# Graph attention on one core: maxima over two rounds, V over dead K, three banks of sums

## The reference

```python
q = (feats @ Wq.T + bq).reshape(bs, NHEAD, HDIM).transpose(1, 0, 2)   # k, v alike
qe = q[:, c, :]; ke = k[:, r, :]; ve = v[:, r, :]                     # one row per edge
sim = jnp.einsum('hed,hed->eh', qe, ke) * scale
m = jax.ops.segment_max(sim, c, num_segments=bs)                      # per node and head
p = jnp.exp(sim - m[c])
s = jax.ops.segment_sum(p, c, num_segments=bs)
attn = p / s[c]
agg = jax.ops.segment_sum(attn.T[..., None] * ve, c, num_segments=bs) # reshaped to 256
return agg @ Wo.T + bo
```

## Time and profile before

| What | Value |
|---|---|
| Median of three runs | 6950.24 us (6938.55 to 6957.0) |
| The profiled execution | 6949.4 us |
| Its span, first to last instruction | 6947.6 us |
| First `product` (L1670) | starts at 3812.0 us |
| Last `product` | starts at 6702.6 us |
| Last `add` (L1716) | starts at 6742.6 us |
| Busy over the whole span | PE 65%, DVE 65%, ACT 57%, POOL 67% |

### The profile page before, as it was taken

One profiled execution on the slowest core, in us unless ns is written; L12 is line 12 of the kernel. 1 busy time (PEld: TensorE's weight loads), 2 busy tenths in 40 slices (PEclk: granted clock), 3 DMA queues, 4 the chain that ended last, 5 costly groups with the idle time before them and its releaser, 6 DMA issues. The chain is left out here.

```text
span 6947.6 us, 117508 instructions
## 1 busy us (share of the span) xinstructions
PE 4531.6 (65%) x19717; PEld 3355.2 (48%) x19717; DVE 4539.1 (65%) x12295; ACT 3956.7 (57%) x14482; POOL 4638.8 (67%) x3716
## 2 busy tenths in 40 slices
PE   1366666666666666664886677777677777777767
PEld 1344444444444545543553555555555555555545
DVE  4565555555556666663554777777777777777766
ACT  0665555555555555552332667677676767677661
POOL 1478888888888888887554566666666666666630
PEclk6677777777777777776998888888888888788889
DMA  8767777777777777778774566666666666676746
GB/s 314 188 105 106 104 107 106 106 107 106 106 106 109 107 109 107 110 108 184 263 260 144 167 183 190 188 195 187 199 190 198 197 196 201 199 206 202 206 145 196
DMA packets 644181, 1130.07 MB, mean 163 GB/s; under 512 B 74529, under 2 KB 466795, under 8 KB 643445
## 3 DMA queue, kind: packets, MB, share of 16 engines
q0 software_dynamic: 367600, 678.97, 49.7%
q1 hardware_dynamic: 223985, 273.78, 12.1%
q10 hardware_dynamic: 51860, 169.74, 7.4%
HBM read 929.80 MB, written 451.51 MB: 199 GB/s over the span
## 5 line engine op out<-in xcount | busy, mean ns | idle before, releaser
L701 POOL DMA_INDIRECT sums<-mtw,posIw x1563 | 2489.4, 1593 | 599.1 <-issue 408.2
L1249 POOL DMA_INDIRECT kv<-kvt,sI x1760 | 1763.8, 1002 | 1044.0 <-ACT room L1613 654.3
L1613 ACT ACTIVATE room<-kv,pp 128x33 f32<-128x33 f32 x8800 | 1918.1, 308 | 42.3 <-issue 38.1
L1528 PE MATMUL ps<-room,Of 128*128 128x264 f32 x3520 | 1143.0, 467 | 611.5 <-issue 339.3
L734 PE MATMUL ps<-h,wf 128*128 x3320 | 1212.0, 518 | 303.3 <-DVE mtw L825 230.6
L718 PE MATMUL ps<-Mw,Oh 128*128 128x128 f32 x3320 | 672.7, 368 | 926.9 <-DVE Oh L852 926.9
L825 DVE SCALAR_TENSOR_TENSOR mtw<-mtw,cont,ps 128x256 f32 x1660 | 794.2, 478 | 619.2 <-SPq L690 452.1
L1528 PEld LDWEIGHTS ps<-room,Of 128*128 128x128 f32 x3520 | 727.3, 224 | 890.7 <-issue 618.2
L718 PEld LDWEIGHTS ps<-Mw,Oh 128*128 128x128 f32 x3320 | 630.1, 274 | 1041.7 <-DVE Oh L852 1011.7
L734 PEld LDWEIGHTS ps<-h,wf 128*128 128x128 f32 x3320 | 805.8, 260 | 590.8 <-issue 455.3
L799 ACT COPY wf<-ps 128x512 f32<-128x512 f32 x415 | 242.7, 585 | 1238.8 <-PE ps L718 870.3
(11 more groups left out here) (223 smaller groups left out, 4509.3 us busy)
## 6 DMA issues: line engine op xcount, KB each, us to landing
qb<-qt SPq DMA_DIRECT2D x880, 192.0 KB
accd<-acc SPq DMA_DIRECT2D x880, 132.0 KB
ints<-srows ACTq DMA_DIRECT2D x205, 512.0 KB
OT<-drows SPq DMA_DIRECT2D x110, 512.0 KB
sums<-zero ACTq DMA_DIRECT2D x72, 704.0 KB
part<-sums SPq DMA_DIRECT2D x56, 896.0 KB
kv<-kvt,sI POOLq DMA_INDIRECT x1760
kvt<-kvo SPq DMA_DIRECT2D x98, 260.0 KB
```

The source lines that it names most:

```text
L701: e.indirect_dma_start(sums[t % NS], bass.IndirectOffsetOnAxis(ap=posI[:, t % NP:t % NP + 1], axis=0), mt[:, t % NM, :], None, compute_op= ...
L1249: e.indirect_dma_start(kv[:, s % NK, :], None, kvt, bass.IndirectOffsetOnAxis(ap=sI[:, s:s + 1], axis=0)).then_inc(kvs.sem(s), 16)
L1528: m = e.matmul(psum[6 + j % 2][:, 0:NH * 33], lhsT=Of[:, w % 2, k % W2, :], rhs=pv[:, k % NV, :], start=(k % 2 == 0), stop=(k % 2 == 1))
L1613: e.activation(pv[:, s % NV, h * 33:h * 33 + 33], kv[:, s % NK, D + h * 33:D + h * 33 + 33], ACT.Copy, scale=pp[:, w % 2, h, s % W2:s % W2 ...
```

## The change

It does five things, all in the attention stage.

1. **The chain takes two rounds.** `turn` of round w-1 and `spread` of round w-2 share PE's step u = 0; `ends` of w-1, `back` and `factor` of w-2 share u = 2. DVE does `inner` of w-1 and `outer` of w-2 at u = 1, `across` of w-1 at u = 3. ACT takes `exps` of w-2, the tops of w-1 and the factor of w-2 at u = 3, and a copy of the transposed similarities (`zs`) and the limits at u = 1. `sims` has three places in place of two.
2. **One bank for the chain.** All its results lie in bank 4, so PE waits before it writes there until ACT has read what lay there. ACT now copies the transposed similarities (`zs`) and the factor (`fac`) to SBUF, two new copies per round; the scans and `rescale` read these.
3. **Later weighing.** Weighing of quad Q comes in step Q+11, `agg` in Q+12, `add` in Q+13 (STEPS = 440 + 13).
4. **Three banks of sums.** Banks 5, 6 and 7: `agg` of sum j waits for the `add` of sum j-3.
5. **V on dead K.** `kv` is 12 columns of 7 x 264 floats. Successive rows of one column lie 264 floats lower, so that a row's V covers the K of the row gathered 12 slots before. The gather of quad g waits for the product of quad g-3, and for the weighing of quad g-15. 12 slots are gathered ahead of the stage, in place of 24. ACT raises its semaphore once per slot, not once per head, and POOL no longer waits row by row.

```diff
-        NK, NQ, RB, NE = 44, 8, 8, 24
+        NQ, RB = 8, 8
+        CH, VP, HW = 12, 6, NH * 33
+        NE = CH
...
+        kvs = Ring(sw[0:11], 4)
...
+        def lot(s):
+
+            return VP - s // CH % VP
+
+        def keys(s, n):
+            return kv[:, s % CH:s % CH + n, lot(s) * HW - D:lot(s) * HW]
+
+        def values(s, n):
+            return kv[:, s % CH:s % CH + n, lot(s) * HW:(lot(s) + 1) * HW]
 
         def gather(e, s):
 
-            e.indirect_dma_start(kv[:, s % NK, :], None, kvt, bass.IndirectOffsetOnAxis(
+            e.indirect_dma_start(kv[:, s % CH, lot(s) * HW - D:(lot(s) + 1) * HW], None, kvt, bass.IndirectOffsetOnAxis(
                 ap=sI[:, s:s + 1], axis=0)).then_inc(kvs.sem(s), 16)
 
...
-                e.wait_ge(S("l_wact"), NH * weighed(1, Q))
+                e.wait_ge(S("l_wact"), weighed(1, Q))
...
                                         ALU.mult).then_inc(S("l_wpool"), 1)
 
                 e.iota(icolI[:, :], pattern=[[0, 1]], base=0, channel_multiplier=1).then_inc(S("l_iota"), 1)
-                for g in range(NQD + 10):
-                    if g >= 10:
-                        weigh(g - 10)
-                    if g < NQD:
-                        if g >= NK // 4:
-                            wait_weighed(e, g - NK // 4)
-                        for s in range(max(NE, 4 * g), 4 * g + 4):
-                            if g >= NK // 4 and s % 4:
-                                before = NH * weighed(1, g - NK // 4)
-                                e.wait_ge(S("l_wact"), before + s % 4 * NH * len(shares(g - NK // 4 + 1)[1]) // 4)
+                for g in range(NQD + 14):
+                    if g >= 14:
+                        weigh(g - 14)
+                    if CH // 4 <= g < NQD:
+                        e.wait_ge(S("l_prod"), g - CH // 4 + 1)
+                        if g >= (VP - 1) * CH // 4:
+                            wait_weighed(e, g - (VP - 1) * CH // 4)
+                        for s in range(4 * g, 4 * g + 4):
                             gather(e, s)
 
...
-                        if j >= 2:
-                            e.wait_ge(S("l_add"), j - 1)
+                        if j >= 3:
+                            e.wait_ge(S("l_add"), j - 2)
                         for k in (2 * j, 2 * j + 1):
-                            m = e.matmul(psum[6 + j % 2][:, 0:NH * 33], lhsT=Of[:, w % 2, k % W2, :], rhs=pv[:, k % NV, :],
+                            m = e.matmul(psum[5 + j % 3][:, 0:NH * 33], lhsT=Of[:, w % 2, k % W2, :], rhs=pv[:, k % NV, :],
                                          start=(k % 2 == 0), stop=(k % 2 == 1))
                         m.then_inc(S("l_summed"), 1)
...
                 for p in range(STEPS):
                     w, u = p // 4, p % 4
-                    if u == 0:
-                        factor(w - 2)
                     expand(p + 1)
                     if u == 0:
+                        if 0 <= w - 2 < NW2:
+                            e.wait_ge(S("l_top"), w - 1)
+                        if 0 <= w - 3 < NW2:
+                            e.wait_ge(S("l_pp"), w - 2)
+                            e.wait_ge(S("l_fac"), w - 2)
                         turn(w - 1)
-                    elif u == 1:
+                        spread(w - 2)
+                    elif u == 2:
+                        if 0 <= w - 1 < NW2:
+                            e.wait_ge(S("l_z"), w)
+                        if 0 <= w - 2 < NW2:
+                            e.wait_ge(S("l_lim"), w - 1)
                         ends(w - 1)
-                    elif u == 2:
-                        spread(w - 1)
-                    else:
-                        back(w - 1)
-                    agg(p - 8)
+                        back(w - 2)
+                        factor(w - 2)
+                    agg(p - 12)
...
                         for h in range(NH):
-                            e.activation(pv[:, s % NV, h * 33:h * 33 + 33],
-                                         kv[:, s % NK, D + h * 33:D + h * 33 + 33], ACT.Copy,
-                                         scale=pp[:, w % 2, h, s % W2:s % W2 + 1]).then_inc(S("l_wact"), 1)
-
...
+                            m = e.activation(pv[:, s % NV, h * 33:h * 33 + 33], from_row[:, h * 33:h * 33 + 33], ACT.Copy,
+                                             scale=pp[:, w % 2, h, s % W2:s % W2 + 1])
+                        m.then_inc(S("l_wact"), 1)
...
+
+                def factor(v):
+                    if 0 <= v < NW2:
+                        e.wait_ge(S("l_factor"), v + 1)
+                        if v:
+                            e.wait_ge(S("l_rescale"), v)
+                        e.copy(fac[:, :], chain[:, fcol]).then_inc(S("l_fac"), 1)
+
+                def turned(v):
+                    if 0 <= v < NW2:
+                        e.wait_ge(S("l_ts"), v + 1)
+                        if v >= 2:
+                            e.wait_ge(S("l_bw2"), v - 1)
+                        e.copy(zs[:, v % 2, :], chain[:, zcol]).then_inc(S("l_z"), 1)
...
+                for p in range(STEPS):
+                    w, u = p // 4, p % 4
+                    if u == 3:
+                        if 0 <= w - 1 < NW2:
+                            e.wait_ge(S("l_tops"), w)
+                        if 0 <= w - 2 < NW2:
+                            e.wait_ge(S("l_factor"), w - 1)
+                        exps(w - 2)
+                    weigh(p - 11, 0)
+                    if u == 1:
+                        if 0 <= w - 2 < NW2:
+                            e.wait_ge(S("l_sides"), w - 1)
+                        turned(w - 1)
+                        limits(w - 2)
+                    if u == 3:
+                        ends(w - 1)
+                        factor(w - 2)
+                    weigh(p - 11, 1)
...
-                    add(p - 9, 0)
+                    add(p - 13, 0)
                     reduce(p)
-                    add(p - 9, 1)
+                    add(p - 13, 1)
+                    weigh(p - 11)
                     if u == 0:
                         columns(w + 1)
-                        rescale(w - 2)
+                        onehots(w - 2, 0)
+                        rescale(w - 3)
+                    elif u == 1:
                         inner(w - 1)
-                    elif u == 1:
-                        weigh(p - 7)
+                        outer(w - 2)
+                    elif u == 2:
+                        onehots(w - 2, 1)
+                    else:
                         across(w - 1)
-                    elif u == 2:
-                        weigh(p - 7)
-                        onehots(w - 1, 0)
-                        outer(w - 1)
-                    else:
```

91 lines of the change are left out of this document (41 added, 50 removed).

## The result

Over four runs each the changed kernel takes 7127.66 us (7096.73 to 7142.33) and the kernel before 6951.26 (6938.55 to 6957.0): a ratio of 1.025, with a 95% interval of 1.021 to 1.029. The forecast was 6566 us. The profiled execution took 7096.73 us, its span 7094.8.

A forecast was written before the change was run, and what follows sets the result against it. No engine is full; late PE results hold the 26.5 us round, above POOL's 21.0 us floor. Forecast: 6949.4 - 418 (110 rounds, 26.5 to 22.7 us) + 35 for the stage's ends = 6566 us, range 6390 to 6880.

The forecast's parts named there:

- the waits before the scans: DVE's idle time before across, inner and outer, 310.5 us or 3.2 us per round, was to go.
- the slack of the sums: Three banks give PE's two sums per step 7.2 and 5.1 us to spare; a 9.1 us delay leaves 4.0 idle.
- I price them at nothing: PE's new waits on ACT were to cost nothing; if ACT runs a step later, add waits up to 5.1 us.
- R: The new round of the attention stage, taken as 22.7 us where it was 26.5; its range 21.8 to 23.7.
- the fill: Start of the stage: with 12 slots gathered ahead, not 24, the first quads save less, costing +16 us.
- The drain: End of the stage: four more quads of weighing at 4.7 us of ACT each, +19 us.
- The floor: POOL's lowest round: 16 gathers 1.25 us apart and one weighing, 21.0 us.
- the case in which delays vanish: Rival: no delay of PE's results passes its slack, so R is 21.0 us and time 6379 us; chance 0.15.
- The one in which waits move to the sums in every round: Rival: every round has one 9.1 us delay on the sums, R 24.3 us, time 6742 us; chance 0.24.
- The slower rival, the gate of the gathers: Rival: POOL, at most three quads ahead, stands 5.7 us per round for the product; R 26.7, 7006 us; chance 0.12.
- The delay that I couldn't explain: PE's results reach ACT 6.3 and DVE 9.1 us late while gathers stream, and come through when POOL pauses.
- The rule on two SBUF operands: DVE instructions with two SBUF inputs and POOL's weighing shut each other out, about 0.5 us per round; left out of the sum.

The follow-up runs named there:

- chip 4: Another chip with held results, where the changed kernel was rerun against the kernel before: 7123.55 us beside 7003.57, ratio 1.0168.
- chip 7: A chip where nothing is held, where the changed kernel was run against the kernel before: 6428.96 us beside 6350.44, ratio 1.0129.
- lead2: Changed kernel with gathers waiting for the product two quads ahead, not three: 7165.88 us, against 7123.55 for the changed kernel on that chip.

## Why the prediction was wrong

**Right: the waits before the scans go.** 310.5 us before, none now.

**The step that failed: the slack of the sums, and "I price them at nothing".** I gave each sum at least 5.1 us to spare, the first of a step 7.2, against a delay of 9.1 us, and so 4.0 us of waiting in half of the rounds. I priced PE's new order at nothing, since behind the chain's matmuls "stands only `agg`". That was the point. In PE's step u = 2 the two sums now come behind `ends`, `back` and `factor`, and these wait for the scans at the end of DVE's step u = 1 (L1847 ends at 5011.90 in the timeline above, the sums start at 5013.14). I had the first sum of a step end 1.0 us before the start of the product; in this step it ends 2.5 us after it. From the records of the trace (4000 to 6600 us), each `add` set beside its own sum: the first `add` of DVE's step u = 3, which needs that sum, has a median slack of 3.3 us. It waits over 1 us in 71 of 94 rounds, 6.8 us on average, and starts then a median of 11.6 us after PE is done. This one `add` per round has 484 of the 599 us. In all, 83 of 94 rounds wait over 1 us at some `add`, 7.2 us on average. So three sizes were off: the slack (3.3, not 7.2 or 5.1), the delay (11.6, not 9.1) and how often (nearly all rounds, not half). And I had no term for the product: 1.4 us a round. Measured are 6.4 us before `add` and 1.4 before the product; with 20.1 us of work they make the 28.0 us.

**In the sum.** R is 27.96 in place of 22.7 us, which is 110 x 5.26 = 578 us. The ends gave 48 us less than I had (below). 6566 + 578 - 48 = 7096 is the profiled execution; the median of the four runs lies 31 us higher, which makes up the miss of 562.

**What `pp` is not.** ACT's 699.3 / 93 = 7.5 us a round before `pp` look like the cause, since the weighing of a round follows directly behind. But of the 598.6 us that DVE waited before `add`, 598.5 came after PE had finished the sum (by the modelled ends of matmuls), and a sum started a median of 2.4 to 10 us after its quad had been weighed, by its place in the round. On chip 4, 458 of 471 us came after. So the late weighing isn't what DVE waited for. ACT has 19.1 us of work in a round of 28, and rests where its order makes it wait. No run gave `pp` or the sums of u = 2 more slack, so this rests on the accounts of the traces and not on an experiment.

**Open: why the delay is longer, and where it falls.** Counted from the end of the sum on PE, the `add`s that waited over 1 us had a median delay of 8.1 us and 11.7 at most before; now it is 11.0 and 12.6 at most. On chip 4 the `add` named above has only 150 of the 471 us, the others share the rest, and the median delay is 6.0 us (12.8 at most). So which sum is held, and how long, differs between the two chips; that DVE waits for finished sums holds on both. What the traces have on the cause stands below.

**Wrong: the fill.** +35 us were to come from the ends. The drain was near (+19 expected, +15.9 and +18.5 measured). The fill was not: instead of costing 16 us, the first product comes 16.8 us earlier, and the first quads save 30 us against steady rounds where they had saved 21. The first of these fits the 12 gathers fewer ahead of the product, 1.25 us each or 15 us; I had counted the missing slots only as a loss. With the measured R my formula gives 7145, 48 us over the profiled execution.

**The floor.** 21.0 us per round for POOL was meant as the case in which delays vanish. The runs on chip 7 show that case: R is 21.3 before and 21.7 now. I had taken 1.25 us from gather to gather, two undisturbed ones, for both kernels; on average it is 1.29 and 1.32 there, and on the chip of the result a gather now takes 1069 ns and the floor would be 22.5. With 110 x 0.4 and nothing for the ends the kernel would take 6394 us on chip 7; with the +61.8 of the products 6412; measured are 6429. The rest is in the choice of traces: the two profiled executions are 53 us apart, the medians 78.

**The rivals.** The one in which waits move to the sums in every round (R = 24.3, 6742 us) named the place and the frequency, and had 4.0 us for what measured 7.8. The sign that I gave for being wrong, rounds as long as before with the idle time moved to `add`, is what came. The slower rival, the gate of the gathers (7006 us), had the nearest time with another mechanism: POOL does stand for the product (337.7 us), but no product of the stretch waits for a gather to land, one quad of lead is worth 0.4 us a round (lead2), and the gate on the kernel before cost 6 to 15 us in all where nothing is held. It wasn't run alone where results are held, and whether its stops and starts lengthen the holds is open.

**The delay that I couldn't explain.** I wrote that results come late while gathers stream and come through when POOL pauses. The first half stands, the second does not: in the timeline above `pp` is released at 5019.80 with POOL in the middle of its stream. Over all holds above 2.5 us (4000 to 6000 us, from the records of the transfers): on chip 4, during the 50 at `pp` the gathers' transfers fill 0.69 of the DMA engines, and 0.33 in the 1.5 us behind the release; in the kernel before, for the 43 at the tops, 0.70 and 0.33. That looks like a release in a lull. On the chip of the result the 62 at `pp` have 0.66 and 0.61, so there it is not so; at `add` it is 0.69 and 0.43. What ends a hold is not shown. Lulls have become fewer: taking as dense each stretch in which the gathers fill over 0.45 of the DMA engines (three slices of half a microsecond averaged), the mean stretch from 4000 to 6600 us is 5.2 to 5.3 us before and 7.0 to 7.3 now on these two chips; 18% of all time lay in stretches over 10 us, now 36 to 37%. That fits longer holds. It is an observation on four traces and no experiment: on chip 7 the transfers are denser still (the median stretch is 19 us) and nothing is held. Why chips differ so, no run here tells.

**The rules drawn on.** By the Trainium skill, "SBUF — State Buffer", section "SBUF: two separate sides", transfers and engines can't slow each other, which I gave to the rival of vanishing delays. In data no run contradicts it: a product lasts as long on either kind of chip (medians of 1211 to 1224 ns). But the delays did not vanish. The products of the kernel before span 2890.6 us on the chip of the result and 2316.3 on chip 7, 574 us or 5.2 us a round less; of DVE's idle time there are 6.2 us a round on the one and 1.3 on the other, so most of the difference goes with the holds. The rule on two SBUF operands, at 55 us, can't be seen in POOL's weighing, which became shorter (813 to 642 ns).
